# Gathers of a chunk in parts of five, each part begun when the one before it has landed

## The reference

```python
h = x @ node_w.T                              # (12500, 64)
rf = edge_attr_64 @ review_w.T                # (400000, 64)
m = (h[src] + rf) * edge_weight1
agg = jax.ops.segment_sum(m, dst, num_segments=12500)
return layernorm(x + agg, axis=-1)            # eps 1e-5, no scale or shift
```

## Time and profile before

| | us |
|---|---|
| time, median of 2 runs | 2815.59 |
| lowest and highest of them | 2814.23, 2816.95 |
| span of the profiled execution, first to last instruction | 4978.1 |
| PE busy in it | 2706.6 (54%) |
| POOL busy | 2097.5 (42%) |
| DVE busy | 1848.4 (37%) |
| ACT busy | 832.4 (17%) |
| mean granted TensorE clock in it | 0.722 |

### The profile page before, as it was taken

The page is one execution under the profiler, slowest core; times in us unless marked ns, Lnnn a source line. Parts: engine busy times, 40 slices in busy tenths (PEclk is TensorE's granted clock), DMA queues, the critical chain, the costliest instruction groups (busy, mean ns, idle before and its releaser), DMA issues.

```text
span 4978.1 us, 63532 instructions
## 1 busy us (share of the span) xinstructions
PE 2706.6 (54%) x22003; PEld 2036.4 (41%) x22004; DVE 1848.4 (37%) x7016; ACT 832.4 (17%) x1327; POOL 2097.5 (42%) x2223
## 2 busy tenths in 40 slices
PE   0555555545655545555456555555554556455465
PEld 0343444434443434444344434344443444344345
DVE  3333333423442333333334424333333344333344
ACT  0111111111121111121111211111111112111112
POOL 7343343443334443444433344434444333544432
PEclk9776777767776767777667767677776777667677
DMA  4111121111111111211111211112111112112111
GB/s 98 37 34 37 34 42 38 34 36 38 37 38 38 34 35 38 41 38 34 35 38 35 42 37 35 34 38 42 38 34 35 37 36 42 37 34 43 36 35 38
DMA packets 531458, 192.11 MB, mean 39 GB/s; under 512 B 489893, under 2 KB 495772, under 8 KB 530975
## 3 DMA queue, kind: packets, MB, share of 16 engines
q1 hardware_dynamic: 334128, 80.80, 8.6%
q0 software_dynamic: 70400, 72.23, 6.6%
q10 hardware_dynamic: 126623, 34.94, 3.2%
HBM read 184.60 MB, written 3.20 MB: 38 GB/s over the span
## 4 chain that ended last, share of the span: by engine, by line
PE 43%; another core or an unknown queue 28%; issue 21%; DVE 4%; ACT 2%; DVEq 1%; ACTq 1%; POOLq 0%; POOL 0%
PE x_sums_ps L896 15%; PE count_ps L881 15%; PE window_ps L839 11%; ACT counts L744 2%; DVE scatter L441 1%; DVE hot_lo L497 1%; PE attr_ps L873 1%; ACTq L771 0%; PE turn_ps L858 0%; PE turn_ps L855 0%; DVEq L422 0%; DVEq L425 0%; DVE hot_key L495 0%; PE count_ps L924 0%
## 5 line engine op out<-in xcount | busy, mean ns | idle before, releaser
L366 POOL DMA_INDIRECT rows<-x,src x2200 | 2088.8, 949 | 2791.5 <-DMA src<-src 2146.3
L881 PE MATMUL count_ps<-hot_key,hot_lo 128*128 128x343 bf16 x5550 | 1157.4, 361 | 1294.2 <-ACT counts L744 839.0
L896 PE MATMUL x_sums_ps<-counts,x_tab 128*64 128x126 f32 (+1 forms) x10192 | 865.5, 302 | 790.2 <-issue 775.0
L881 PEld LDWEIGHTS count_ps<-hot_key,hot_lo 128*128 128x128 bf16 x5550 | 570.1, 113 | 1726.5 <-issue 1092.5
L896 PEld LDWEIGHTS x_sums_ps<-counts,x_tab 128*64 128x64 f32 x10192 | 692.5, 154 | 948.4 <-issue 927.3
L744 ACT ACTIVATE counts<-count_ps 128x686 f32<-128x686 f32 x925 | 737.3, 802 | 1784.9 <-remote 1335.6
L495 DVE TENSOR_SCALAR hot_key<-count,cols 128x686 bf16<-128x686 f16 x925 | 377.8, 408 | 1550.8 <-remote 1272.3
L441 DVE TENSOR_SCALAR scatter<-column,dst_left,w 128x128 f32<-128x128 f32 x2200 | 588.3, 347 | 576.2 <-PE window_ps L839 503.0
L497 DVE TENSOR_SCALAR hot_lo<-count,cols 128x128 bf16<-128x128 f16 x2775 | 721.7, 323 | 4.9 <-issue 4.9
L839 PE MATMUL window_ps<-scatter,rows 128*128 128x128 f32 x4400 | 563.1, 289 | 85.2 <-issue 55.4
L839 PEld LDWEIGHTS window_ps<-scatter,rows 128*128 128x128 f32 x4400 | 535.0, 200 | 120.9 <-issue 108.8
(11 more groups left out here) (112 smaller groups left out, 557.5 us busy)
## 6 DMA issues: line engine op xcount, KB each, us to landing
rows<-edge_attr SPq DMA_DIRECT2D x88, 800.0 KB
rows<-x,src POOLq DMA_INDIRECT x2200
g_attr<-edge_attr ACTq DMA_DIRECT2D x51, 576.0 KB
out<-x_tab SPq DMA_DIRECT2D x11, 256.0 KB
counts<-dst SPq DMA_DIRECT2D x1, 1562.5 KB
src<-src SPq DMA_DIRECT2D x88, 12.5 KB, 1.7
dst<-dst SPq DMA_DIRECT2D x88, 12.5 KB
w<-edge_weight SPq DMA_DIRECT2D x88, 12.5 KB
```

The source lines that it names most:

```text
L366: pool.indirect_dma_start(out=rows[:, s, k, 0:F], out_offset=None, in_=x, in_offset=bass.IndirectOffsetOnAxis(ap=src_sb[s][:, k:k + 1].bit ...
L881: last = pe.matmul(count_ps[b][:, a, 0:HALF], hot_lo[h][:, i, :], hot_key[h][:, a * HALF:(a + 1) * HALF], start=(i == 0), stop=(i == 2))
L896: done = pe.matmul(x_sums_ps[half * F:(half + 1) * F, 0:ns], x_tab[:, hi, :], counts[:, hi, 0:ns], start=(hi < 2), stop=(hi >= HI - 2))
```

## The change

Inside a chunk's 25 gathers, before the 6th, 11th, 16th and 21st, POOL waits until the five gathers before have all landed (80 on that part's semaphore for each chunk that used the slot), and adds one more to `gathers_begun`. The first five gathers of a chunk wait for nothing new, and nothing waits for the last five on POOL. No other engine's stream is touched.

```diff
                 pool.sem_inc(gathers_begun, 1)
                 for k in range(TILES):
+                    if k and k % PER_PART == 0:
+                        pool.wait_ge(gathered[s][k // PER_PART - 1], (r + 1) * (16 * PER_PART))
+                        pool.sem_inc(gathers_begun, 1)
                     pool.indirect_dma_start(
                         out=rows[:, s, k, 0:F], out_offset=None, in_=x,
                         in_offset=bass.IndirectOffsetOnAxis(ap=src_sb[s][:, k:k + 1].bitcast(U32), axis=0),
```

## The result

The changed kernel takes 3582.8 us (median of 2 runs, 3577.26 to 3588.33) against 2815.59: the ratio is 1.273, with an interval of 1.268 to 1.278. That is 767 us more, slower by 27%; forecast were 635 us more and 3450 us, in a range of 3190 to 3640.

A forecast was written before the change was run, and what follows sets the result against it. The prediction took POOL's string of gathers to bound the timed kernel. To the median of 2815.6 us it added 352 waits at 1.85 us (651 us), less 16 us slack: 3450 us, range 3190 to 3640.

The forecast's parts named there:

- Rivals 1 and 2: Waits hidden by POOL's slack: wholly, time stays at 2815 us (chance 0.05); half, step 1.10 us, 3094 us (chance 0.05).
- The reason given for the 4978: Profiled span of 4978.1 us against a 2815.6 us median: POOL's extra slack was taken to belong to the profiled execution.
- rival 3: Gathers in flight hold back PE, ACT and DVE; drains save at most 144 us: 2671 us; chance 0.02.
- The step: POOL's time from one gather to the next: 0.949 us of gather plus a 0.305 us pause, about 1.25 us.
- the 33 us: Gap between POOL's summed 2783 us and the timed median, left to time around a launch's span and occasional waits.
- the 16 us: POOL's assumed slack in the timed runs, half of 0 to 33 us, subtracted from the added wait time.
- The drain: Each POOL wait for the five gathers before: 1.85 us beyond the usual pause, 352 times, 651 us.
- (a): In a drain, from the end of the fifth gather's instruction until its data has moved: 1.2 us.
- (b): In a drain, from landing to the start of the waiting gather: 0.85 us, read from a chunk's `src` load.
- PE's clock: PE might lose clock speed while waiting: 2190 us over 0.7 is 3130 us, under 3450; nothing counted for it.

The follow-up runs named there:

- increments-only: The changed kernel without its four waits per chunk, keeping the four increments: 2812.9 us beside 2813.0 for the kernel before, ratio 1.000.
- lagging wait: Changed kernel, but waits before the 11th, 16th, 21st gather, for the five before the last five: ratio to kernel before 1.0013 (2816.6 us), later 1.0018 (4994.7 us).

## Why the prediction was right, and where it was off

**The bound: right for the timed pair.** POOL's string of gathers bounds the timed kernel before. The increments-only profile shows the chain (75% gathers, 24% pauses). Rivals 1 and 2 of the prediction, waits that are hidden wholly or half, fall: one drain per chunk costs 182 us, when 2.2 us of slack per chunk would have hidden it.

**The reason given for the 4978: wrong.** The prediction had "the slack of the profile is the profiled execution's own". It is not the profiler's: on the free chip the profiled run of the increments-only kernel took 2813.76 us with a span of 2812.0, beside nine more of 2810 to 2813; on a held chip the profiled run of the lagging wait took 4996.92, beside nine more of 4980 to 4999. The number that saved the forecast was the timed median, not the trace. The prediction carried POOL's string over to 2815 because the step of 1.25 us is the same in both kinds; that holds. But the sentence that the profiled span "may move far less than the timed run, or not at all" fell with the reason. On a held chip it fell by a quarter, and the timed run with it. So the forecast is right for the free kind alone: on a held chip the same edit has the other sign, which only rival 3 had, with a small price.

**The step: 1.254 us forecast from the trace, 1.267 on a free chip** (2788.2 over 2200). The mean gather is 962 ns there, not 949; why was not tested. That is 28 of the 33 us that the prediction had left over and took for slack. The slack is nil, and the 16 us taken off for it were wrong.

**The drain: the term that was undersized.** Forecast 1.85 us over the pause that stood there, measured 2.54 - 0.305 = 2.235. Two parts: a quiet hole is 2.31 us, so 2.0 over the pause where 1.75 was worked out, 352 x 0.25 = 90 us; and the long holes add 0.23 a wait in place of 0.1, 46 us. The pieces (a) and (b) can now be measured, the landing on the 132 of the 352 drained gathers for which the profile has one. The last packet of the fifth gather ends 1.18 us (median) after its instruction; the windows of data movement had given 1.2, and that was right. The landing counts 0.33 us later, 1.5 after the instruction's end and 2.5 after its start: this piece was missing in the sum. POOL goes on 0.80 us after the landing, where the `src` load had given 0.85. The sum closes: 635 + 90 + 46 + 16 for the slack, less 13 because the gathers themselves were a little shorter (957 ns against 962), is 774, as the two spans differ (3586.4 - 2812.0); the runs differ by 767.

By the Trainium skill (DMA: Bandwidth & Descriptors, Anatomy of one DMA), 2.0 us fixed and the bytes give, as an estimate, 2.08 us for a gather. The run says 2.5 from the start of the instruction (2.3 the least), and 1.5 from its end. Counted from the start the estimate is 0.4 low, counted from the end 0.6 high; neither reading fits, and the measurement stands.

**PE's clock: no part in it.** The mean granted clock is 0.801 in the changed kernel and 0.906 in the increments-only one, and PE has 0% of either chain.

**Rival 3: its mechanism is real, and its price was not.** On held chips gathers that go on without a break do hold back PE, ACT and DVE in timed runs. It was given 0.02 and at most 144 us, worked out against 2815. (The step that it needs comes out of its own numbers as 0.91 us, not 0.92; nothing hangs on it.) On a free chip there is no drag to win back (ratio 1.27). On a held chip it is worth 1230 us (ratio 0.75).

One correction to the description of the kernel: the loop makes nine rounds of five steps, not ten; the other six steps are written out.

## What to carry to other kernels

Where an engine issues one short transfer after another without a pause, and this string is the bound, a wait for the newest costs the whole way of a landing each time (2.2 us here, 27% of the kernel); one for a transfer some steps back costs next to nothing (ratio 1.0013). When a profile's span and the timed runs differ by far, find out first whether the kernel has two times: run it on more than one chip before the trace is explained, and judge a change on both kinds. This one costs 27% on the one and gains 25% on the other, and a gap in the string of gathers makes that gain, while a cap of ten in flight does not.

## What the runs showed that was not expected

- The kernel before takes 2813 us on one chip and 4928 to 4992 us on three others. In the held kind PE, ACT and DVE are slowed down from some 4 us into a string of gathers (PE's busy share ends at 0.12 to 0.17) until 4 to 5 us after the last gather of a string of 25, 2 to 3 us after one of ten, and POOL's own step stays at 1.25 us. Gaps of about 2.1 to 2.3 us after every fifth gather bring it to 3698 to 3804 us.
- What part of the chip does this was not found. Bulk loads are not it (ratio 0.748 without most of them, 0.751 with), nor does a cap of ten gathers in flight help (1.0018).
- A gather that lands beside a bulk load of `edge_attr` can take far longer than the rest: in the changed kernel the landing is 2.3 us at least, 2.5 in the median and 8.7 at most (880 of the 2200 gathers have one in the profile). With the bulk loads light the holes of the changed kernel are 2.43 us in the mean, with them 2.65, on one chip. Where the drains stand also counts: two per chunk cost 2.87 us each on the free chip, one 2.43, and 46 of the 176, but 3 of the 88, had 200 KB or more of loads beside them.
